# News product of the steady slots on VectorE instead of GpSimd: a recurrent network kernel

## Chip, cores and metric

The kernel runs on one core of a Trainium2 chip. The metric is the time of one execution in microseconds (us) on the device. Five engines work in order, each through its own list of instructions: TensorE (matmuls), VectorE and GpSimd (elementwise), ScalarE (activations) and SyncE (which only issues DMAs here). They meet at semaphores: an instruction behind `wait_ge(s, n)` starts once semaphore s has reached n, and `.then_inc(s, 1)` raises it when an instruction is complete. SBUF is the memory in which all engines but SyncE work on tiles of 128 partitions; PSUM, the tensor `ps` of eight banks, is where TensorE writes, and GpSimd does not use it.

## The reference

For 2048 rows with 50 time steps of 128 features, and one further vector `news` per row:

```
h_t  = GRU(x_t, h_{t-1})                      z, r = sigmoid(...), hc = tanh(xh + r*hh)
                                              h = z*h + (1-z)*hc
emb  = [h_t, news - h_t, news, h_t * news]
at   = sigmoid(relu(relu(emb W1 + b1) W2 + b2) W3 + b3)          attention score per step
g_t  = second GRU over h_t, its update gate multiplied by at:    u = sigmoid(...), r = sigmoid(...)
                                              c = tanh(xc + r*(g Uc)), g = (1 - at*u)*g + at*u*c
y    = sigmoid(dense(leaky(dense(leaky(batchnorm([g_T, news]) ...)))))
```

`h_t * news` is the product that the change is about.

## The kernel before

Features lie on the 128 partitions, and the 2048 rows are four chunks (NC) of 512 columns. An item is one chunk of one time step: 4 x 50 = 200 items, item i having chunk i % 4. Matmuls run in float16, each operand split into a high and a low part (`h_hi`, `h_lo`); a product of weights and data is three passes (high with high, high with low, low with high) over two halves of 64 output rows, six matmuls (`split_product`, L1149 and L1150 of `two_tiles`). ScalarE makes the high parts, GpSimd or VectorE the low ones by a subtraction.

The program is written as slots, by hand, for each engine. Slot `low` does the first GRU for item `low`, the first attention layer for item `low` - 2, and the second GRU for item `low` - 10 (LAG). Slots 4 to 13 are the function `early`; slots 14 (EARLY) to 199 are `slot`, the steady ones; after them ten slots of `late` finish the second GRU, and the dense layers end the kernel. In every fourth steady slot (17, 21, ... 197) TensorE also does the second attention layer (`attention_2`, L1232) and the scores (`scores`, L1223), and ScalarE and VectorE have work for these at the beginning of the slot behind (L575, L581, L856).

A steady slot, in order, on each engine, with the names by which the rows call the results:

- TensorE: attention layer 1 on h and on h*news (waits for `h_lo`, `hn_lo`), reset gate of item `low`, update gate of the second GRU (waits for the new h of item `low` - 1, which frees its bank), `xh`, second GRU's reset gate and its `ghh`, the update gate z, `gxh` (waits for the second state g), in every fourth slot the scores (`pe.wait_ge(gr_ready, late(LAG))`: their bank is the one that `gr` is read from) and the second attention layer, then `hh` of a later item.
- ScalarE: [relu and high part of the second attention layer], candidate of the second GRU L662, `h_hi` L502, `r` L647, `a_hi` L512, `hn_hi` L507, `gu` L676, `x_hi` L527, `hc` L686, `g_hi` L690, `gr` L693, z L696.
- VectorE: [`a_lo` L856], `ps` L861 (attention plus its share of the news), `ps` L879, [`a_lo` L856], `t` L988 (waits for r), `ps` L885 (waits for `gus`), `t` L998, `g` L890, `a_lo` L867, `gt` L1027 (waits for gr), `ps` L1033 (waits for `d` and z), `gt` L1038, `h` L1041, the new state of item `low`. Then the next slot's list begins.
- GpSimd: `g_lo` L409, `hn` L327 of item `low` - 1 (`state_news`, waits for h), `gus` L416 (update gate times score), `hn_lo` L333 (waits for ScalarE's `hn_hi`), `h_lo` L339, `d` L423 (waits for hc), `x_lo` L346.
- SyncE: the loads of x for the next step and the rows of scores, each behind its semaphore.

`hn` has two buffers, one for even and one for odd items. In `late(ITEMS)`, the first slot behind the steady ones, GpSimd makes `gus` and then the `hn` of the last item, item 199, before `h_lo` and `hn_lo` of it.

Of the kernel before, what the change touches and what calls it, by code (L numbers as in the profile page):

```python
# [24 lines left out]
ALU = mybir.AluOpType  # L25
# [8 lines left out]
NC = 4  # L34
# [43 lines left out]
def rec_kernel(nc, xs, pack_gru, pack_state, pack_att, pack_rest, out):  # L78
# [21 lines left out]
    def has(item):  # L100
        return 0 <= item < ITEMS
# [26 lines left out]
    with ExitStack() as ctx:  # L128
# [187 lines left out]
        def _(pool):  # L316
# [4 lines left out]
            def state_news(item, count):  # L321

                c, k = item % NC, item % 2
                if isinstance(item, int) and item < NC:
                    pool.wait_ge(news_landed[c], 16)
                pool.wait_ge(h_ready, count)
                g.tensor_tensor(hn[:, k, :], h32[:, c, :], news[:, c, :], ALU.mult).then_inc(hn_ready, 1)  # L327
# [69 lines left out]
            def slot(s0, off):  # L397
                low = off + (s0 if isinstance(s0, int) else LOOP_LO)

                def at(lag):  # L400
                    return s0 + (off - lag + 1)

                def landed(lag):
                    return 4 * (s0 + (off - lag - (low - lag) % NC)) + 16

                if has(low - LAG - 4) and has(low - LAG - 4 + NC):
                    c = (low - LAG - 4) % NC
                    pool.wait_ge(ghi_ready, at(LAG + 4))
                    g.tensor_tensor(g_lo[:, c, :], g32[:, c, :], g_hi[:, c, :], ALU.subtract).then_inc(glo_ready, 1)  # L409
                if has(low - 1):  # L410
                    state_news(low - 1, at(1))
                if has(low - LAG - 1):
                    c, k = (low - LAG - 1) % NC, (low - LAG - 1) % 2
                    pool.wait_ge(gu_ready, at(LAG + 1))
                    pool.wait_ge(score_landed, landed(LAG + 1))
                    g.tensor_tensor(gus[:, k, :], gu[:, k, :], score[:, c, :], ALU.mult).then_inc(gus_ready, 1)  # L416
                if has(low - 1):
                    state_news_low(low - 1, at(1))
                    state_low(low - 1, at(1))
                if has(low):  # L420
                    c, k = low % NC, low % 2
                    pool.wait_ge(hc_ready, at(0))
                    g.tensor_tensor(d[:, k, :], h32[:, c, :], hc[:, k, :], ALU.subtract).then_inc(d_ready, EARLY + 1 if low == EARLY else 1)  # L423
                if has(low + 1) and low > EARLY:
                    input_low(low + 1, at(-1))
# [13 lines left out]
            def late(low):  # L439
                item = low - LAG  # L440
                if low == ITEMS:
                    gated_low(item - 4)
                if item >= ITEMS - LAG + 2:
                    pool.wait_ge(ge_ready, item - 2 - NC)
                gated_share(item - 1, item, 16 * ((item - 1) // NC + 1), score if item <= ITEMS - 2 * NC else late_scores[(item - 1) // NC - T + 2])
                if low == ITEMS:
                    state_news(ITEMS - 1, ITEMS)
                if low == ITEMS:
                    state_low(ITEMS - 1, ITEMS)
                    state_news_low(ITEMS - 1, ITEMS)  # L450
                    gated_low(item - 3)
                elif low <= SHORT + 1:
                    gated_low(item - 3 if low <= SHORT else item - 2)
                if SHORT <= low < LAST - 1 and low != SHORT + 1:
                    gated_low(item - 2)
                if ITEMS + 3 <= low < ITEMS + 3 + NC:
                    c = low - ITEMS - 3
                    pool.wait_ge(newshi_ready, c + 1)
                    g.tensor_tensor(news_lo[:, c, :], news[:, c, :], news_hi[:, c, :], ALU.subtract).then_inc(newslo_ready, 1)
                if low == ITEMS + 2:  # L460
                    pool.wait_ge(d1_half, 1)
                    g.tensor_tensor(d1_lo, dw1, d1_hi, ALU.subtract).then_inc(d1_split, 1)
                    pool.wait_ge(d2_half, 1)
                    g.tensor_tensor(d2_lo, dw2, d2_hi, ALU.subtract).then_inc(d2_split, 1)
# [349 lines left out]
        def _(dve):  # L814
# [152 lines left out]
            def slot(s0, off):  # L967
                low = off + (s0 if isinstance(s0, int) else LOOP_LO)

                def at(lag):  # L970
                    return s0 + (off - lag + 1)

                def late(lag):
                    return s0 + (off - lag + 1 - NC)

                if pairs_of(low - 1):
                    low_2(0, paired(s0 + (off - 1)))
                if has(low - 2):
                    attention_1_news(low - 2, at(2))
                if low > EARLY and has(low - LAG - 1):  # L980
                    gated_difference(low - LAG - 1, at(LAG + 1))
                if low > EARLY and pairs_of(low - 1):
                    low_2(1, paired(s0 + (off - 1)))
                if has(low):
                    k = low % 2
                    dve.wait_ge(hh_pe, late(0))
                    dve.wait_ge(r_ready, at(0))
                    v.scalar_tensor_tensor(out=t[:, k, :], in0=ps[:, B_HH, :], scalar=b_hs,  # L988
                                           in1=r[:, k, :], op0=ALU.add, op1=ALU.mult).then_inc(t1_ready, 1)
                if low == EARLY:  # L990
                    gated_first(low - LAG - 1, at(LAG + 1))
                elif has(low - LAG - 1):
                    gated_step(low - LAG - 1, at(LAG + 1))
                if has(low):
                    k = low % 2
                    dve.wait_ge(t1_ready, at(0))
                    dve.wait_ge(xh_pe, at(0))
                    v.tensor_tensor(t[:, k, :], t[:, k, :], ps[:, B_XH, :], ALU.add).then_inc(t2_ready, 1)  # L998
                if low == EARLY:
                    low_2(1, paired(low - 1))  # L1000
                if low > EARLY and has(low - LAG - 1):
                    gated_state(low - LAG - 1, at(LAG + 1))
                if has(low - 2):
                    attention_1_low(low - 2, at(2))
                known = low if isinstance(s0, int) else None
                if known == BN_LO:
                    bn_eps()
                if known == BN_LO + 1:
                    bn_guess()
                for i in range(NEWTON):  # L1010
                    if known == BN_LO + 3 * i + 2:
                        bn_square(i)
                    if known == BN_LO + 3 * i + 3:
                        bn_error(i)
                    if known == BN_LO + 3 * i + 4:
                        bn_root(i)
                if known == BN_LO + 3 * NEWTON + 2:
                    bn_scale()
                if known == BN_LO + 3 * NEWTON + 3:
                    bn_mean()  # L1020
                if known == BN_LO + 3 * NEWTON + 4:
                    bn_shift()
                if has(low - LAG):
                    k = (low - LAG) % 2
                    dve.wait_ge(ghh_pe, late(LAG))
                    dve.wait_ge(gr_ready, late(LAG))
                    v.tensor_tensor(gt[:, k, :], gr[:, k, :], ps[:, B_GHH, :], ALU.mult).then_inc(gt1_ready, 1)  # L1027
                if known == BN_LO:
                    bn_shift_bits()
                if has(low):  # L1030
                    dve.wait_ge(d_ready, at(0))
                    dve.wait_ge(z_ready, at(0))
                    v.tensor_tensor(ps[:, B_Z, :], d[:, low % 2, :], ps[:, B_Z, :], ALU.mult).then_inc(e_ready, 1)  # L1033
                if has(low - LAG):
                    k = (low - LAG) % 2
                    dve.wait_ge(gxh_pe, at(LAG))
                    dve.wait_ge(gt1_ready, late(LAG))
                    v.tensor_tensor(gt[:, k, :], gt[:, k, :], ps[:, B_GXH, :], ALU.add).then_inc(gt2_ready, 1)  # L1038
                if has(low):
                    dve.wait_ge(e_ready, at(0))  # L1040
                    v.tensor_tensor(h32[:, low % NC, :], hc[:, low % 2, :], ps[:, B_Z, :], ALU.add).then_inc(h_ready, 1)  # L1041

            dve.wait_ge(gru_landed, 16)
            v.tensor_tensor(b_zr[:, :], gru_b[:, 0:2], gru_b[:, 3:5], ALU.add).then_inc(b_ready, 1)
# [543 lines left out]
```

## Time and profile before

| | |
|---|---|
| time, median of 3 runs | 1918.23 us (1917.87 to 1918.46) |
| the profiled execution: its own time | 1917.94 us |
| its span | 1916.1 us |
| granted TensorE clock | 1.0 of full |
| busy PE / DVE / ACT / POOL | 1908.0 / 1473.6 / 1471.6 / 1645.4 us |
| hn L327 on POOL | 200 times, mean 1275 ns |
| h L1041 on DVE | 186 times, mean 681 ns |

The profile calls the engines PE (TensorE), PEld (its weight loads), DVE (VectorE), ACT (ScalarE), POOL (GpSimd) and SP (SyncE). Busy time is time in which an instruction of the engine is being executed, as the record of start and end has it; a time in which the instruction waits within the engine for something that is no semaphore counts as busy. An engine at 77% with others at 100% says nothing by itself: what matters is whose wait ends last at the place in question.

### The profile page before, as it was taken

Reading aid. Unit: us, or ns where it says so; the run is one execution under the profiler, and the core shown is the slowest. Engines: PE = TensorE matmul, PEld = TensorE weight load, DVE = VectorE, ACT = ScalarE, POOL = GpSimd, SP = SyncE. Lnnn points to the kernel's source line nnn. Section 1 sums busy time; section 2 is a strip of 40 time slices with the busy share of each in tenths; the row PEclk is TensorE's granted clock in tenths of the full one; section 3 lists DMA queues with packets and bytes.
Section 4 is the critical chain, followed back from the end, with each engine's and each line's share of the span. In section 5 each row is a group of like instructions: output and inputs, shape, how many; then the busy total and the mean of one; then the engine's idle time right before and its main releaser. Section 6 shows DMA issues by size and latency. Waiting matters only on the chain.

```text
span 1916.1 us, 44510 instructions
## 1 busy us (share of the span) xinstructions
PE 1908.0 (100%) x17607; PEld 999.3 (52%) x17607; DVE 1473.6 (77%) x2324; ACT 1471.6 (77%) x2484; POOL 1645.4 (86%) x1409
## 2 busy tenths in 40 slices
PE   9999999999999999999999999999999999999999
PEld 4555555555555555555555555555555555555554
DVE  7777777777777777777777777777777777787777
ACT  7877777777777777777777777777777777777777
POOL 7888888888888888888888888888888888888886
PEclk9999999999999999999999999999999999999999
DMA  4211121112111211121121112111211121112110
GB/s 131 69 55 53 55 69 54 51 51 73 51 51 51 73 51 50 54 70 50 51 69 55 50 51 73 51 54 53 70 53 51 51 73 51 51 51 73 45 46 23
DMA packets 37911, 110.67 MB, mean 58 GB/s; under 512 B 4348, under 2 KB 4732, under 8 KB 31304
## 3 DMA queue, kind: packets, MB, share of 16 engines
q1 hardware_dynamic: 37560, 107.57, 17.4%
q8 instruction: 140, 2.29, 0.5%
q14 instruction: 67, 0.55, 0.1%
q10 hardware_dynamic: 144, 0.26, 0.1%
HBM read 107.40 MB, written 0.42 MB: 56 GB/s over the span
## 4 chain that ended last, share of the span: by engine, by line
PE 94%; ACT 2%; DVE 1%; POOL 1%; issue 1%; DMA 0%; SPq 0%; DVEq 0%; ACTq 0%; POOLq 0%
PE ps L1149 88%; PE ps L1232 3%; PE ps L1150 1%; PE ps L1223 1%; POOL hn_lo L333 0%; POOL h_lo L339 0%; DMA x<-in_xs 0%; DVE ps L885 0%; DVE ps L879 0%; ACT ps L752 0%; POOL hn L327 0%; ACT ps L575 0%; ACT g_hi L736 0%; ACT a_hi L512 0%; DVE g L890 0%
## 5 line engine op out<-in xcount | busy, mean ns | idle before, releaser
L1149 PE MATMUL ps<-h_hi,w_hi 128*64 128x512 f16 x1384 | 524.6, 379 | 1.9 <-POOL h_lo L339 1.4
L1150 PE MATMUL ps<-h_hi,w_hi 128*64 128x512 f16 x1384 | 524.7, 379 | 0.0
L1150 PE MATMUL ps<-h_lo,w_hi 128*64 128x512 f16 x1384 | 524.5, 379 | 0.0
L1150 PE MATMUL ps<-h_hi,w_lo 128*64 128x512 f16 x1384 | 524.5, 379 | 0.0
L1149 PE MATMUL ps<-h_hi,w_lo 128*64 128x512 f16 x1384 | 524.5, 379 | 0.0
L1149 PE MATMUL ps<-h_lo,w_hi 128*64 128x512 f16 x1384 | 524.5, 379 | 0.0
L333 POOL TENSOR_TENSOR hn_lo<-hn,hn_hi 128x512 f16<-128x512 f32 x200 | 232.4, 1162 | 162.2 <-ACT hn_hi L507 161.8
L327 POOL TENSOR_TENSOR hn<-h,news 128x512 f32<-128x512 f32 x200 | 255.0, 1275 | 74.3 <-DVE h L1041 74.3
L662 ACT ACTIVATE ps<-gt,p_rest 128x512 f32<-128x512 f32 x185 | 127.7, 690 | 199.4 <-DVE gt L1038 199.4
L346 POOL TENSOR_TENSOR x_lo<-x,x_hi 128x512 f16<-128x512 f32 x196 | 226.9, 1158 | 11.8 <-ACT x_hi L527 11.8
L416 POOL TENSOR_TENSOR gus<-gu,score 128x512 f32<-128x512 f32 x186 | 237.0, 1274 | 0.0
L423 POOL TENSOR_TENSOR d<-h,hc 128x512 f32<-128x512 f32 x186 | 236.8, 1273 | 0.0
L1027 DVE TENSOR_TENSOR gt<-gr,ps 128x512 f32<-128x512 f32 x186 | 128.0, 688 | 138.5 <-ACT gr L693 138.5
L339 POOL TENSOR_TENSOR h_lo<-h,h_hi 128x512 f16<-128x512 f32 x200 | 233.2, 1166 | 0.4 <-ACT h_hi L502 0.3
L1149 PE MATMUL ps<-x_hi,w_hi 128*64 128x512 f16 x605 | 229.3, 379 | 0.6 <-DVE a_lo L856 0.6
L1150 PE MATMUL ps<-x_hi,w_hi 128*64 128x512 f16 x605 | 229.3, 379 | 0.0
L1149 PE MATMUL ps<-x_lo,w_hi 128*64 128x512 f16 x605 | 229.3, 379 | 0.0
L1150 PE MATMUL ps<-x_lo,w_hi 128*64 128x512 f16 x605 | 229.3, 379 | 0.0
L1149 PE MATMUL ps<-x_hi,w_lo 128*64 128x512 f16 x605 | 229.3, 379 | 0.0
L1150 PE MATMUL ps<-x_hi,w_lo 128*64 128x512 f16 x605 | 229.3, 379 | 0.0
L1149 PEld LDWEIGHTS ps<-h_hi,w_hi 128*64 128x64 f16 x1384 | 152.2, 110 | 146.1 <-issue 3.0
L1149 PE MATMUL ps<-g_hi,w_hi 128*64 128x512 f16 x596 | 225.9, 379 | 1.1 <-DVE g_lo L1097 1.1
(191 smaller groups left out, 6756.4 us busy)
## 6 DMA issues: line engine op xcount, KB each, us to landing
x<-in_xs SPq DMA_DIRECT2D x199, 256.0 KB, 3.0
score<-score_rows SPq DMA_DIRECT2D x48, 1024.0 KB, 4.7
news<-in_xs SPq DMA_DIRECT2D x4, 256.0 KB, 5.3
x<-score_rows SPq DMA_DIRECT2D x1, 1024.0 KB, 4.6
h<-score_rows SPq DMA_DIRECT2D x1, 1024.0 KB, 5.1
score_rows<-s_rows SPq DMA_DIRECT2D x50, 8.0 KB
p_rest<-in_pack_rest SPq DMA_DIRECT2D x1, 776.0 KB, 7.0
p_att<-in_pack_att SPq DMA_DIRECT2D x1, 291.0 KB, 5.3
```

What stands on the lines that cost most here:

```text
L327: g.tensor_tensor(hn[:, k, :], h32[:, c, :], news[:, c, :], ALU.mult).then_inc(hn_ready, 1)
L333: g.tensor_tensor(hn_lo[:, item % NC, :], hn[:, k, :], hn_hi[:, item % NC, :], ALU.subtract).then_inc(hnlo_ready, 1)
L339: g.tensor_tensor(h_lo[:, item % HIST, :], h32[:, c, :], h_hi[:, item % HIST, :], ALU.subtract).then_inc(hlo_ready, 1)
L346: g.tensor_tensor(x_lo[:, c, :], x32[:, c, :], x_hi[:, c, :], ALU.subtract).then_inc(xlo_ready, 1)
L416: g.tensor_tensor(gus[:, k, :], gu[:, k, :], score[:, c, :], ALU.mult).then_inc(gus_ready, 1)
L423: g.tensor_tensor(d[:, k, :], h32[:, c, :], hc[:, k, :], ALU.subtract).then_inc(d_ready, EARLY + 1 if low == EARLY else 1)
L662: a.activation(ps[:, B_GXH, :], gt[:, (low - LAG - 1) % 2, :], ACT.Tanh, bias=b_gated[:, 2:3]).then_inc(gc_ready, 1)
L1027: v.tensor_tensor(gt[:, k, :], gr[:, k, :], ps[:, B_GHH, :], ALU.mult).then_inc(gt1_ready, 1)
L1149: m.matmul(ps[0:H, bank, :], weights[:, 0:H], moving, start=start, stop=stop)
L1150: return m.matmul(ps[H:P, bank, :], weights[:, H:P], moving, start=start, stop=stop)
L1223: done = m.matmul(ps[p * H:(p + 1) * H, bank, :], w3_pair[:, :], part[:, p, :], start=part is a2_hi, stop=part is a2_lo)
L1232: done = m.matmul(ps[k * H:(k + 1) * H, B_PAIR[p], :], w[:, A_2, 0:H], a1[:, 2 * p + k, :], start=w is w_hi and a1 is a1_hi, stop=a1 is a1_lo)
```

## The change

In the steady slots 14 to 199 VectorE multiplies the state with the news. The product stands directly behind the new state h of the same slot, so it is that of item `low` in slot `low`, where GpSimd made that of item `low` - 1. GpSimd keeps the products up to that of item 13, which it makes in slot 14; items 14 to 199, 186 of them, are VectorE's, item 199 in slot 199. VectorE waits for the low part of item `low` - 2 (it frees the buffer of hn), and for its own h.

```diff
@@ GpSimd, slot
-                if has(low - 1):
+                if low == EARLY:
                     state_news(low - 1, at(1))
@@ GpSimd, late
-                if low == ITEMS:
-                    state_news(ITEMS - 1, ITEMS)
                 if low == ITEMS:
                     state_low(ITEMS - 1, ITEMS)
                     state_news_low(ITEMS - 1, ITEMS)
@@ VectorE, slot
                 if has(low):
                     dve.wait_ge(e_ready, at(0))
                     v.tensor_tensor(h32[:, low % NC, :], hc[:, low % 2, :], ps[:, B_Z, :], ALU.add).then_inc(h_ready, 1)
+                    if low == EARLY:
+                        dve.wait_ge(hn_ready, low)
+                    dve.wait_ge(hnlo_ready, at(2))
+                    dve.wait_ge(h_ready, at(0))
+                    v.tensor_tensor(hn[:, low % 2, :], h32[:, low % NC, :], news[:, low % NC, :], ALU.mult).then_inc(hn_ready, 1)
```

## Rows read from the trace of the kernel before

**Rows 1.** The page, part 1: busy us (share of the span) xinstructions.

```profile
PE 1908.0 (100%) x17607; PEld 999.3 (52%) x17607; DVE 1473.6 (77%) x2324; ACT 1471.6 (77%) x2484; POOL 1645.4 (86%) x1409
```

**Rows 2.** Waits of TensorE, longest: waiter <- releaser: us in total, times, longest us.

```profile
PE ps L1149 <- POOL h_lo L339: 1.4, 1, 1.4
```

**Rows 3.** Chain that ended last: start us, us, what; first and last of 46 such pieces.

```profile
122.92 1.29 PE ps L1232 x12
...
1832.32 1.29 PE ps L1232 x12
```

**Rows 4.** Timeline of VectorE: start us, us, engine, line, operation, out<-in [idle before <-releaser].

```profile
1017.40 0.68 DVE L1041 TENSOR_TENSOR h<-hc,ps 128x512 f32<-128x512 f32 x1
1018.02 0.70 DVE L861 TENSOR_TENSOR ps<-c_news,ps 128x512 f32<-128x512 f32 x1
...
1020.12 0.75 DVE L988 SCALAR_TENSOR_TENSOR t<-ps,p_gru,r 128x512 f32<-128x512 f32 x1 [0.80 <-ACT r L647]
...
1021.38 0.68 DVE L998 TENSOR_TENSOR t<-t,ps 128x512 f32<-128x512 f32 x1
...
1024.01 0.69 DVE L1027 TENSOR_TENSOR gt<-gr,ps 128x512 f32<-128x512 f32 x1 [0.75 <-ACT gr L693]
...
1025.86 0.68 DVE L1038 TENSOR_TENSOR gt<-gt,ps 128x512 f32<-128x512 f32 x1
1026.46 0.68 DVE L1041 TENSOR_TENSOR h<-hc,ps 128x512 f32<-128x512 f32 x1
```

**Rows 5.** Timeline of GpSimd in the same slot.

```profile
1018.16 1.27 POOL L327 TENSOR_TENSOR hn<-h,news 128x512 f32<-128x512 f32 x1 [0.40 <-DVE h L1041]
1019.39 1.27 POOL L416 TENSOR_TENSOR gus<-gu,score 128x512 f32<-128x512 f32 x1
1021.08 1.16 POOL L333 TENSOR_TENSOR hn_lo<-hn,hn_hi 128x512 f16<-128x512 f32 x1 [0.42 <-ACT hn_hi L507]
1022.20 1.16 POOL L339 TENSOR_TENSOR h_lo<-h,h_hi 128x512 f16<-128x512 f32 x1
1023.32 1.27 POOL L423 TENSOR_TENSOR d<-h,hc 128x512 f32<-128x512 f32 x1
1024.55 1.15 POOL L346 TENSOR_TENSOR x_lo<-x,x_hi 128x512 f16<-128x512 f32 x1
1025.67 1.16 POOL L409 TENSOR_TENSOR g_lo<-g,g_hi 128x512 f16<-128x512 f32 x1
```

**Rows 6.** Timelines of head and tail: VectorE's two-tensor operations and GpSimd's beside them.

```profile
19.61 1.27 POOL L327 TENSOR_TENSOR hn<-h,news 128x512 f32<-128x512 f32 x1
...
20.05 1.38 DVE L1056 TENSOR_TENSOR x_lo<-x,x_hi 128x512 f16<-128x512 f32 x1 [1.42 <-ACT x_hi L527]
...
20.84 1.60 POOL L339 TENSOR_TENSOR h_lo<-h,h_hi 128x512 f16<-128x512 f32 x1
...
1900.52 0.61 POOL L468 CAST a_hi<-r 128x512 f16<-128x512 f32 x1
...
1900.53 1.14 DVE L1097 TENSOR_TENSOR g_lo<-g,g_hi 128x512 f16<-128x512 f32 x1 [0.19 <-ACT g L737]
```

**Rows 7.** Timeline of VectorE, two operations, the second waiting for the first.

```profile
79.33 0.69 DVE L955 TENSOR_TENSOR d<-d,ps 128x512 f32<-128x512 f32 x1
80.06 0.69 DVE L957 TENSOR_TENSOR h<-d,ps 128x512 f32<-128x512 f32 x1
```

**Rows 8.** Timeline of ScalarE in the slot of rows 4.

```profile
1019.90 0.59 ACT L512 ACTIVATE a_hi<-ps 128x512 f16<-128x512 f32 x1
1020.38 0.63 ACT L507 ACTIVATE hn_hi<-hn 128x512 f16<-128x512 f32 x1
...
1022.09 0.72 ACT L686 ACTIVATE hc<-t,p_gru 128x512 f32<-128x512 f32 x1
...
1023.24 0.67 ACT L693 ACTIVATE gr<-ps,p_rest 128x512 f32<-128x512 f32 x1
```

**Rows 9.** Timeline of TensorE: the first score matmuls of the slot behind.

```profile
1034.00 0.38 PE L1223 MATMUL ps<-a_hi,w_pair 128*64 128x512 f16 x2
```

## The prediction

> **What bounds the kernel now.** I read the busy table first: TensorE is busy for 1908.0 of 1916.1 us, so at most 8.1 us of the span are anything but matmuls [rows 1]. Next the waits: the longest that TensorE has is 1.4 us, once, for an h_lo [rows 2]; the slots of the loop appear in none of its rows. The chain repeats every four slots: the twelve score-layer matmuls stand in it from 122.92 to 1832.32 us, 46 times, which is 1709.40 / 45 = 37.99 us for four slots [rows 3]. A plain slot takes 9.06 us (the new h from 1017.40 to 1026.46) [rows 4]; the fourth, in which TensorE has the second attention layer and the scores besides, takes 37.99 - 3 x 9.06 = 10.8. I call it the score slot. The change can win something only in head or tail; in the loop it can lose, if a ring of waits over the other engines becomes longer than 37.99.
>
> **What is removed.** GpSimd loses 186 multiplications (items 14 to 199) of 1.27 us, and with each the wait for h: h ends at 1018.08, hn starts at 1018.16 [rows 4, 5]. That is 236 us of GpSimd time, none of it in the chain of the loop. The one that GpSimd makes in slot 14 stays. The last one, behind the steady slots, brought h_lo and hn_lo of one item up to 1.2 us later; TensorE did not wait there, so the gain lies between 0 and 1.4 us (its longest wait, rows 2). I take 0.
>
> **What is added.** VectorE gets one 128x512 multiplication per slot, of two SBUF operands. Its operations in the loop take 0.68 to 0.75 and start some 0.60 apart [rows 4]. Taken at 0.60 it would be hidden: t starts at 1020.12, set by the reset gate; from h at 1017.40 come h, ps, ps at 0.62, 0.60 and 0.60, so 0.9 us before t were free, of which 0.3 would be left. No DMA is added and none is moved.
>
> But no operation of VectorE in the loop reads two SBUF tensors, since one operand always lies in ps, and the few of head and tail that do are the slow ones [rows 6]. At 20.05 VectorE's x_lo begins while GpSimd's hn runs to 20.88; it ends at 21.43, so it takes 1.38, and ends 0.55 behind the end of GpSimd's operation. GpSimd's next, h_lo, begins in the record at 20.84, later than VectorE's, and takes 1.60 instead of 1.16: it stood behind VectorE. At 1900.53 VectorE asks 0.01 behind a cast of 0.61 that GpSimd began at 1900.52, and takes 1.14: it stood behind the cast. Who comes first goes first, and the other waits for the whole operation. The Trainium skill says it so too (SBUF — State Buffer, "SBUF: two separate sides": the port pair that the two share is an exclusive lock for the whole instruction, also against a VectorE operation with two SBUF inputs); the trace agrees, with 0.55 us behind the end. By another of its rules (GPSIMD Engine Reference, "Engine selection": elementwise work on a tile belongs on VectorE, GpSimd being about twice as slow) the result would be the hidden 0.60 and no change; its ratio fits 1.27 against 0.68 here, but the shared port is not in it.
>
> **Who comes first.** GpSimd has no late input between g_lo and gus, so gus starts 1.11 us behind g_lo (as g_lo behind x_lo, 1024.55 to 1025.67, rows 5). In an undisturbed slot g_lo starts 9.06 before 1025.67, at 1016.61, and gus at 1017.72. h starts at 1017.40, and an operation that waits for the one before it on VectorE starts 0.73 behind that one's start [rows 7]: hn comes at 1018.13. gus is first by 0.4 us and runs to 1018.99. hn ends 0.55 later, at 1019.54, and the operation behind it may start 0.08 before that, 0.47 behind the end of gus (0.60 behind the start of a 0.68 operation is the same 0.08).
>
> From a start of gus, G, two chains run to the next slot's race.
> To the next gus: gus 1.27, 0.47, ps 0.70, handoff 0.03, a_hi to hn_hi 0.48, hn_hi 0.63, handoff 0.07, then on GpSimd without a gap hn_lo, h_lo, d, x_lo, g_lo: 1.12 + 1.12 + 1.23 + 1.12 + 1.11 [rows 4, 5, 8]. Sum 9.35.
> To the next hn: 1.27 + 0.47, two ps of 0.60, t to the second t 1.26, that t 0.68, handoff 0.03, hc to gr 1.15, gr 0.67, handoff 0.10, three starts of 0.60 up to h, 0.73 [rows 4, 7, 8]. Sum 9.36.
> Both are 0.3 longer than the slot, and they end within some 0.02 us of each other. This is where the prediction is decided. Where gus leads again, the next slot begins 0.3 later still. Where hn leads, it waits only for the rest of g_lo, about 0.5 us are spent instead of 1.7, and the delay is gone.
>
> In the first slot gus leads by 0.4; in the second by 0.1 (there h is still held by the update gate of TensorE's time); from the third on by 0.02 or so. I let gus win: nothing that it waits for is late, while hn passes three semaphores, and 0.73 is the shortest that rows 7 allow for one.
>
> **The sum.** In the slot behind a score slot TensorE's extra 1.7 us let the ring catch up, and there its longest way is through hc: 1.27 + 0.47, four starts (a_lo, ps, ps, a_lo) at 0.60, t to second t 1.26, 0.68, 0.03, hc 0.72, handoff 0.08, d, x_lo, g_lo 1.23 + 1.12 + 1.11, sum 10.37 [rows 4, 5, 8]. The ring of four slots is 3 x 9.35 + 10.37 = 38.42, against TensorE's 37.99: 0.43 us each, wherever TensorE is caught by it. It is caught first by the scores at 1034.00 [rows 9], which need gr: gr ended 9.06 behind 1023.24 + 0.67, at 1032.97. After the change G of the score slot is 1017.72 + 9.06 + 0.6 = 1027.38, and gr ends 1.27 + 0.47 + 1.20 + 1.26 + 0.68 + 0.03 + 1.15 + 0.67 = 6.73 later, at 1034.11, past its deadline. The ring then closes, and TensorE stands still for just as much as it is too long. The rounding of ten handoffs puts 0.43 between 0.4 and 0.5; I take 0.45. 46 x 0.45 = 20.7 us. The profiled execution took 1917.94 us for its span of 1916.1, and stands 0.29 under the median of 1918.23; 1917.94 + 20.7 = 1938.6, on the median's scale 1938.9. I forecast 1939.
>
> **Bounds.** A ring has some ten handoffs, each read to 0.02, and the blocked operation's 0.55 rests on two cases: 0.45 may be 0.15 or 0.8, so 7 to 37 us, 1925 to 1955 for this case.
>
> **Rivals.**
> *hn wins the late races, no change.* A lead of 0.02 us can fall the other way. For it: the two sums are equal within their reading. Against it: the semaphores. If hn leads in the score slot or in the one before, the delay never passes 0.3 there, TensorE's slack of 1.0 us at the scores (1034.00 less 1032.97) holds, and the time is 1918 to 1920. It decides from 0.03 us. A block shorter than rows 6 show, or none at all (0.30 for the race, 0.05 for this), would end in the same time, as the 0.60 is then hidden in the 0.9 ahead of t. Together 0.35.
> *A longer ring, much slower.* If each own semaphore adds 0.05 and a blocked operation 0.1, a plain slot of the ring takes 9.5: 3 x 9.5 + 10.55 = 39.05, 1.06 x 46 = 49 us, 1967. For it: GpSimd's five operations and the chain of VectorE leave no gap to hide such additions in. Against it: rows 6 fit 0.55 to the hundredth. 0.07.
> *Faster.* GpSimd's freed time ends a wait of TensorE in the tail: 1.4 us at most, 1916.8, and that is within the 0.2% (3.8 us) under which a measurement of this kernel can't be told from no change. For more, over half of the 8.1 us that are not matmuls would have to go, and most lie ahead of slot 14: 0.02.
>
> The forecast has 0.56. Slower by over 0.2% is 0.56 + 0.07, less 0.02 for a ring that is too long by under 0.08 us: 0.61. Within 0.2%: 0.37. Faster: 0.02. The range goes from the rival without change to the upper part of my case, 1917.5 to 1950.
>
> **What would show it.** VectorE's new multiplication has a mean of 1.4 us or so, not 0.69; gus starts 1.11 behind g_lo, and hn's record ends 0.55 behind that of gus. TensorE waits some 46 times, 0.3 to 0.6 us, for gr of ScalarE ahead of the scores, and the score-layer matmuls stand 38.4 us apart. I am wrong if they stay 37.99 apart; then in one slot of four hn stands ahead of gus and takes under 1.2 us. If hn takes 0.69 throughout, the port is not shared as rows 6 have it.

## The result, and the profile after

The changed kernel takes 1940.64 us (median of 4 runs, 1939.61 to 1942.03), the kernel before 1918.05 beside it: ratio 1.0116, 95% interval 1.0104 to 1.0128. The forecast was 1939. The profiled execution took 1942.03 us, span 1940.2. One execution of the version with an operand in PSUM, further down, took 2511.11 us at a granted clock of 0.753 and is left out of the ratio there. So the change makes the kernel slower, by 22.6 us, and this is how its profile answers the rows of before.

Part 1 of the page, to be read against [rows 1]:

```profile
PE 1918.9 (99%) x17607; PEld 996.9 (51%) x17607; DVE 1749.1 (90%) x2510; ACT 1468.3 (76%) x2484; POOL 1411.5 (73%) x1223
```

VectorE has 186 operations more, but its busy time grew by 275.5 us, 1.48 for each. GpSimd lost 234. The waits of the whole kernel (waiter, releaser: us in total, times, longest) show where TensorE is caught; [rows 2] had nothing of the steady slots:

```profile
POOL hn_lo L333 <- ACT hn_hi L505: 481.2, 194, 3.1
ACT ps L660 <- DVE gt L1036: 207.3, 139, 2.3
DVE gt L1025 <- ACT gr L691: 130.1, 172, 0.9
ACT a_hi L510 <- DVE ps L859: 114.9, 149, 1.6
...
PEld ps L1226 <- ACT gr L691: 35.0, 46, 0.9
PE ps L1226 <- ACT gr L691: 12.9, 45, 0.4
```

The scores' weight loads wait 46 times for gr of ScalarE. Neither figure is the loss: PEld's counts a stretch in which the array still works on earlier matmuls, PE's only the gap behind their modelled ends. The loss is read from the distance of the same instruction, the first weight load of the scores: 122.11 to 1831.50 us before, 125.10 to 1855.80 after, 45 cycles each, so 37.99 and 38.46 us. That is 21.3 us.

Before:

```profile
122.11 0.11 PEld L1223 LDWEIGHTS ps<-a_hi,w_pair 128*64 128x64 f16 x2
...
1831.50 0.11 PEld L1223 LDWEIGHTS ps<-a_hi,w_pair 128*64 128x64 f16 x2
```

After (the figure in brackets is idle time ahead, and what ended it):

```profile
125.10 0.11 PEld L1226 LDWEIGHTS ps<-a_hi,w_pair 128*64 128x64 f16 x2 [0.88 <-ACT gr L691]
...
1855.80 0.11 PEld L1226 LDWEIGHTS ps<-a_hi,w_pair 128*64 128x64 f16 x2 [0.76 <-ACT gr L691]
```

Timelines of VectorE and GpSimd in a score slot, the one behind it, and two plain ones (start us, us, engine, line, operation):

```profile
1002.15 0.68 DVE L1039 TENSOR_TENSOR h<-hc,ps 128x512 f32<-128x512 f32 x1
1002.93 1.77 DVE L1044 TENSOR_TENSOR hn<-h,news 128x512 f32<-128x512 f32 x1
1004.63 0.68 DVE L859 TENSOR_TENSOR ps<-c_news,ps 128x512 f32<-128x512 f32 x1
1005.22 0.69 DVE L877 TENSOR_TENSOR ps<-ps,g 128x512 f32<-128x512 f32 x1
1005.82 0.74 DVE L986 SCALAR_TENSOR_TENSOR t<-ps,p_gru,r 128x512 f32<-128x512 f32 x1
...
1012.29 1.79 DVE L1044 TENSOR_TENSOR hn<-h,news 128x512 f32<-128x512 f32 x1
...
1022.87 1.58 DVE L1044 TENSOR_TENSOR hn<-h,news 128x512 f32<-128x512 f32 x1
...
1032.04 1.77 DVE L1044 TENSOR_TENSOR hn<-h,news 128x512 f32<-128x512 f32 x1
```

```profile
1001.75 1.17 POOL L409 TENSOR_TENSOR g_lo<-g,g_hi 128x512 f16<-128x512 f32 x1
1002.87 1.28 POOL L416 TENSOR_TENSOR gus<-gu,score 128x512 f32<-128x512 f32 x1
1006.53 1.17 POOL L333 TENSOR_TENSOR hn_lo<-hn,hn_hi 128x512 f16<-128x512 f32 x1 [2.38 <-ACT hn_hi L505]
...
1012.25 1.29 POOL L416 TENSOR_TENSOR gus<-gu,score 128x512 f32<-128x512 f32 x1
...
1019.16 1.28 POOL L423 TENSOR_TENSOR d<-h,hc 128x512 f32<-128x512 f32 x1 [0.26 <-ACT hc L684]
...
1022.63 1.27 POOL L416 TENSOR_TENSOR gus<-gu,score 128x512 f32<-128x512 f32 x1
...
1031.99 1.27 POOL L416 TENSOR_TENSOR gus<-gu,score 128x512 f32<-128x512 f32 x1
```

ScalarE between the two, in the first of these slots:

```profile
1005.34 0.60 ACT L510 ACTIVATE a_hi<-ps 128x512 f16<-128x512 f32 x1 [1.05 <-DVE ps L859]
1005.84 0.62 ACT L505 ACTIVATE hn_hi<-hn 128x512 f16<-128x512 f32 x1
```

gus begins 0.06, 0.04, 0.24 and 0.05 us ahead of hn. hn's record then ends 0.55 behind that of gus (1004.70 against 1004.15), as the blocked operations of [rows 6], and the next operation starts 0.48 behind it. There is no idle time between hn and t; the 0.80 that [rows 4] had ahead of t is gone. GpSimd, relieved of a seventh of its work (234 of 1645 us), spends it waiting 2.4 us for hn_hi. This is a ring: gus holds hn, hn holds ps and with it ScalarE's a_hi and hn_hi, hn_hi holds hn_lo and GpSimd's list, and at its end stands the next gus. In the slot behind the score slot its longest way is through hc, for which d waits (0.26). From one gus to the next it takes 9.38, 10.38, 9.36 and (1041.36 - 1031.99) 9.37 us.

TensorE at the place where the ring catches it, in the same slot (the scores' first matmuls; the number before the arrow is idle time ahead):

```profile
1009.66 0.41 PE L1226 MATMUL ps<-a_hi,w_pair 128*64 128x512 f16 x2 [0.27 <-ACT gr L691]
```

```profile
1009.65 0.11 PEld L1226 LDWEIGHTS ps<-a_hi,w_pair 128*64 128x64 f16 x2 [0.75 <-ACT gr L691]
```

Outside the loop little is left: behind the last score load of the loop come 84.6 us before and 84.4 after. Ahead of the first one the profiled run after is 3.0 us later. Of this, 2.1 stands already at 10.29 us against 8.16 (the first weight load of x_hi), in code that both kernels share and far ahead of the first changed slot, so it isn't the change; 2.2 stands at 101.60 against 99.44, and the other 0.8 comes in before the first scores, where the ring closes. That run is also 1.4 above its median. The medians are 22.6 apart, 21.3 of them the loop.

### The profile page after: what moved, and what is told of

The parts are those of the page before. It is cut to its first block and busy times, and to the rows that moved or that the text cites. A ratio compares the mean times of both kernels' runs of the same rounds, so it can differ in the third digit from the quotient of the medians.

```text
span 1940.2 us, 44696 instructions
## 1 busy us (share of the span) xinstructions
PE 1918.9 (99%) x17607; PEld 996.9 (51%) x17607; DVE 1749.1 (90%) x2510; ACT 1468.3 (76%) x2484; POOL 1411.5 (73%) x1223
## 5 line engine op out<-in xcount | busy, mean ns | idle before, releaser
L1044 DVE TENSOR_TENSOR hn<-h,news 128x512 f32<-128x512 f32 x186 | 315.5, 1696 | 19.4
```

The costliest lines, as they stand in the source:

```text
L1044: v.tensor_tensor(hn[:, low % 2, :], h32[:, low % NC, :], news[:, low % NC, :], ALU.mult).then_inc(hn_ready, 1)
```

## The experiments

The theory to be tested has three parts: VectorE's product meets gus at a shared port and waits for all of it; which of the two comes first decides; TensorE loses just what the ring is longer than 37.99 us. The rivals are that VectorE simply has too much to do, and that the late gr ahead of the scores is the cause by itself. All times are medians, each beside runs of the kernel before on the same chip (1918.0 to 1918.3).

**gus behind hn.** One wait added on GpSimd:

```diff
                     pool.wait_ge(score_landed, landed(LAG + 1))
+                    if has(low - 1):
+                        pool.wait_ge(hn_ready, at(1))
                     g.tensor_tensor(gus[:, k, :], ...)
```

(Dots within a line of a diff stand for arguments that are not shown.)

> GpSimd waits for hn of VectorE before it begins gus; nothing else differs from the changed kernel. Port order theory (a gus that begins just ahead of hn holds VectorE back for 1.27 us): hn then never meets gus, takes 0.69 instead of a mean 1.70, gus still ends before hn_hi is there, the four-slot ring falls back under TensorE's 37.99, time 1918 (1917 to 1920). Rival, load on VectorE (one more operation per slot is too much for an engine in line with the others): nothing changes for VectorE's count of operations, 1938 to 1942.

Measured 1918.41, ratio 1.0003 (0.9994 to 1.0012). The whole loss is gone with a wait more and not one operation less. VectorE's and GpSimd's timelines:

```profile
562.60 0.69 DVE L1046 TENSOR_TENSOR hn<-h,news 128x512 f32<-128x512 f32 x1
```

```profile
563.46 1.27 POOL L418 TENSOR_TENSOR gus<-gu,score 128x512 f32<-128x512 f32 x1 [1.28 <-DVE hn L1046]
```

hn takes 0.69, gus begins 1.28 us later than it could, and nobody waits for it. VectorE is at 83%, with the same 2510 operations as the changed kernel. Load on VectorE is refuted, and the order is shown to decide.

**One operand in PSUM.** The diff shows VectorE; TensorE's two waits for h become waits for hn, as said below it:

```diff
-                    v.tensor_tensor(hn[:, low % 2, :], h32[:, low % NC, :], news[:, low % NC, :], ALU.mult).then_inc(hn_ready, 1)
+                    v.tensor_tensor(hn[:, low % 2, :], h32[:, low % NC, :], ps[:, B_Z, :], ALU.mult).then_inc(hn_ready, 1)
```

> hn is h times the PSUM bank of z instead of h times news (the product with news is left out), so VectorE reads only one SBUF tensor; TensorE waits for hn instead of h before it reuses that bank. Port theory: no meeting with GpSimd at all though gus still begins first, hn 0.69, 1918 to 1920. Rival, load or order of VectorE's list: same operation count and size, 1938 to 1942.

Measured 1919.52, ratio 1.0009 (0.9999 to 1.0019). Here gus begins first and runs right through hn:

```profile
572.85 0.69 DVE L1044 TENSOR_TENSOR hn<-h,ps 128x512 f32<-128x512 f32 x1
```

```profile
572.39 1.27 POOL L416 TENSOR_TENSOR gus<-gu,score 128x512 f32<-128x512 f32 x1
```

Same place in the list, same size, and gus runs through the whole of hn (it leads by 0.46, where it led by 0.05 in the changed kernel); the second SBUF operand is gone, and with it the block, which was about 1.1 us in the changed kernel. So what is shared is the way to SBUF of a second operand. The Trainium skill gives this cause (SBUF — State Buffer, "Who interferes with whom": an instruction of VectorE with at most one SBUF input, outside the 2-port perf modes, doesn't contend with GpSimd, one with two contends with a GpSimd operation that reads); the two traces agree, 0.69 against 1.77 us.

**More work on GpSimd.** (The line that declares `idle` is not shown.)

```diff
+                    g.memset(idle[:, :], 0.0)
                     g.tensor_tensor(gus[:, k, :], ...)
```

> A fill of 128x128 (0.20 us in the trace) is added on GpSimd ahead of gus in each steady slot: GpSimd does more work. Port order theory: gus led hn by only 0.04 to 0.06 us in three of four slots, now it comes 0.1 or more behind it, hn waits only for the rest of g_lo or nothing, 1918 to 1921, faster than the changed kernel. Rival, a ring whose length is what counts whoever comes first: 4 x 0.17 longer per four slots, 1940.6 + 46 x 0.68 = 1972.

Measured 1921.43, ratio 1.0018 (1.0009 to 1.0028): 0.4 above the range that I gave, but 19 us faster than the changed kernel though GpSimd does more. The timelines show both outcomes of the race in turn:

```profile
562.53 0.69 DVE L1046 TENSOR_TENSOR hn<-h,news 128x512 f32<-128x512 f32 x1
571.56 1.51 DVE L1046 TENSOR_TENSOR hn<-h,news 128x512 f32<-128x512 f32 x1
580.66 0.69 DVE L1046 TENSOR_TENSOR hn<-h,news 128x512 f32<-128x512 f32 x1
```

```profile
562.64 1.72 POOL L418 TENSOR_TENSOR gus<-gu,score 128x512 f32<-128x512 f32 x1
...
571.25 1.26 POOL L418 TENSOR_TENSOR gus<-gu,score 128x512 f32<-128x512 f32 x1
...
580.75 1.73 POOL L418 TENSOR_TENSOR gus<-gu,score 128x512 f32<-128x512 f32 x1
```

In one slot hn leads by 0.11 and gus is the one that takes 1.72; in the next gus leads by 0.31 and hn takes 1.51. A slot in which hn leads gives the delay back, and as long as the two outcomes alternate, up to slot 183, four slots take 37.97 to 38.01 us (the first four 37.77), from the new h to the new h. The remaining 3 us (its loop is 1712.26 us for 45 cycles against 1709.39) stand at the end. From slot 184 to slot 197 VectorE has one more small operation in each slot, `bn_t` for the batchnorm, between a_lo and gt (in slot 184 two):

```profile
1789.05 1.64 DVE L1046 TENSOR_TENSOR hn<-h,news 128x512 f32<-128x512 f32 x1
...
1824.37 1.19 DVE L925 SCALAR_TENSOR_TENSOR bn_t<-bn_t,p_rest 128x2 f32<-128x2 f32 x1
1825.48 0.68 DVE L1027 TENSOR_TENSOR gt<-gr,ps 128x512 f32<-128x512 f32 x1
...
1828.05 1.65 DVE L1046 TENSOR_TENSOR hn<-h,news 128x512 f32<-128x512 f32 x1
```

```profile
1827.87 1.29 POOL L418 TENSOR_TENSOR gus<-gu,score 128x512 f32<-128x512 f32 x1
```

With it gt starts 1.71 behind a_lo (1823.77) instead of 1.44, so hn comes 0.27 later, and gus leads in every slot from 184 on, here by 0.18. Four slots then take 39.00 us (1789.05 to 1828.05). So the filler helps only while it turns the race; where gus wins all the same, it lengthens the ring, near the 38.46 + 0.68 = 39.14 of the rival.

**hn later in VectorE's list**, behind L877 of the next slot (that of the last item in the first slot of `late`), with no wait beyond its own:

> VectorE makes hn of item low - 1 in slot low behind ps L877, ahead of t, instead of directly behind h; no wait added. In the kernel before, the place ahead of t had 0.8 us idle and gus would be over by then. Port order theory: hn 0.69 and hidden in three of four slots, delays t by at most 0.3 in the slot behind a score slot, where TensorE gives 1.7 back; 1918 to 1920. Rival, load on VectorE: same load, 1938 to 1942.

Measured 1919.31, ratio 1.0006 (0.9996 to 1.0015). Its hn takes 0.68 from 565.36 on, gus having run from 563.86 to 565.13. The same operation on the same engine costs nothing in a place where GpSimd reads nothing.

**A semaphore in place of the port.** VectorE waits for gus:

```diff
+                    if low > EARLY:
+                        dve.wait_ge(gus_ready, at(LAG))
                     dve.wait_ge(hnlo_ready, at(2))
```

> VectorE waits by a semaphore until gus is complete before it begins hn; port order is then fixed, the meeting is gone and only the ring is left, with a handoff of 0.08 and a full start of 0.60 in place of the 0.47 behind gus: 0.21 longer per slot, 0.84 per four slots. Ring theory: TensorE stands for the ring's excess of 0.48 + 0.84 us, 46 x 1.32 = 61, so 1979 (1968 to 1985). Rival, the blocked port itself costs more than standing behind gus would: faster than 1940.

Measured 1973.96, ratio 1.0290 (1.0273 to 1.0307). The same order, made explicit, costs 33 us more than the port does:

```profile
570.17 0.69 DVE L1046 TENSOR_TENSOR hn<-h,news 128x512 f32<-128x512 f32 x1 [1.18 <-POOL gus L416]
570.78 0.69 DVE L859 TENSOR_TENSOR ps<-c_news,ps 128x512 f32<-128x512 f32 x1
```

```profile
568.86 1.27 POOL L416 TENSOR_TENSOR gus<-gu,score 128x512 f32<-128x512 f32 x1
```

L859 starts 0.65 behind the end of gus (570.78 less 570.13) where it started 0.48 behind it in the changed kernel: 0.17 a slot, not the 0.21 that I had put. Four times 0.17 is 0.68, on the excess of 0.47 makes 1.15; hn to hn over four slots is 598.78 - 559.62 = 39.16, an excess of 1.17, and 46 x 1.17 = 54 us are close to the 56 measured. The ring's length is what TensorE pays.

**A shorter hn.**

```diff
-                    v.tensor_tensor(hn[:, low % 2, :], h32[:, low % NC, :], news[:, low % NC, :], ALU.mult)...
+                    v.tensor_tensor(hn[:, low % 2, 0:448], h32[:, low % NC, 0:448], news[:, low % NC, 0:448], ALU.mult)...
```

> hn is made for 448 of its 512 columns (the last 64 are left out), everything else as in the changed kernel. Both chains of the race get shorter by 0.067 us, so gus still leads; the ring of four slots is shorter by 0.27 and its excess over TensorE's 37.99 falls from 0.48 to 0.21: 1918.2 + 46 x 0.21 = 1928 (1925 to 1931).

Measured 1928.9, ratio 1.0056 (1.0041 to 1.0071). The race is as before (gus at 574.94, hn at 574.99, 1.71 us), the loop is (1841.74 - 123.41) / 45 = 38.19 us by the scores' weight loads, where 38.46 - 0.27 = 38.19 was expected.

> hn for 256 of 512 columns (half is left out): the ring of four slots is shorter by 1.07, so below 37.99, though gus still holds hn back in most slots. Ring theory: a floor at the time of the kernel before, 1918 (1917 to 1919), with hn still blocked where gus leads. Rival, each microsecond of the block costs: half of the 22 us, 1929 or more.

Measured 1919.46, ratio 1.0006 (0.9997 to 1.0015). hn still stands behind gus:

```profile
571.94 1.19 DVE L1044 TENSOR_TENSOR hn<-h,news 128x256 f32<-128x256 f32 x1
```

Where nothing holds it, this form takes 0.42, so it ends 0.7 to 0.8 us late in the slots of the loop, and TensorE loses nothing: its loop is 1709.38 us. A block is free as long as the ring stays under TensorE's cycle. Cost by block alone is refuted.

**The scores later.** TensorE's six matmuls of `candidate_state` ahead of the scores instead of behind the second attention layer:

```diff
+                if has(low + 1):
+                    pe.wait_ge(t1_ready, at(0))
+                    candidate_state(low - NC + 1, at(NC - 1))
                 if score_of(low):
...
-                if has(low + 1):
-                    pe.wait_ge(t1_ready, at(0))
-                    candidate_state(low - NC + 1, at(NC - 1))
```

> The changed kernel, with TensorE's six matmuls for hh of a later item put ahead of the scores in every fourth slot, so that the scores begin 0.65 us later and their wait for gr has 0.65 more room. Ring theory: the wait for the scores only shows the ring's excess; with it relieved, TensorE is caught by the next wait (g or gu of the second GRU, or gr with the delay grown by 0.65) and the time stays at 1938 to 1944. Rival, the late gr ahead of the scores is the cause: its lateness of 0.45 us fits into 0.65, so 1918 to 1922.

> The same order of TensorE in the kernel before, to see what the order alone does: both theories 1917 to 1920, since no wait of TensorE had under 1 us of room there.

Measured 1942.66 (ratio 1.0125, 1.0110 to 1.0140) on the changed kernel and 1918.3 (1.0000, 0.9990 to 1.0009) on the one before. The waits of the weight loads, changed kernel with the new order:

```profile
PEld ps L1152 <- DVE g L888: 30.1, 125, 0.3
PEld ps L1152 <- ACT gu L674: 24.5, 102, 0.3
PEld ps L1226 <- ACT gr L691: 10.4, 45, 0.2
```

The wait at which TensorE was caught fell from 35.0 to 10.4 us, two others took its place, and the time did not fall (it is 2 us above that of the changed kernel, within the expected range). The late gr is a symptom.

## Why the prediction was right

- *What bounds it, and that nothing can be won in the loop*: right. Every version whose ring is short enough ends at 1918 to 1920, none below.
- *hn is blocked by gus, 0.55 behind its end*: right, 0.55 in the changed kernel. That the second SBUF operand does it was argued from rows of head and tail; the run with an operand in ps shows it.
- *Who comes first*: the outcome was right, and it was given only 0.56. The two chains were put at 9.35 and 9.36, equal within their reading, so that it came out this way is in part luck: the range, 1917.5 to 1950, took in the other outcome too. gus led by 0.04 to 0.06 in the late races, not 0.02. The term that was short is VectorE's wait for its own h: hn starts 0.78 behind h's start (1002.15 to 1002.93), where [rows 7] gave 0.73. That makes the second chain 9.41. The way in was forecast as leads of 0.4, 0.1 and 0.02; the first four races of the run have 0.98, 0.04, 0.05 and 0.03. The filler, which moves gus by 0.16 us, turns the race in every second slot up to slot 183.
- *The sum*: a ring of 38.42 was forecast, taken as 0.45 over TensorE's 37.99; measured 38.46, so 0.47. Its parts, gus to gus, were 9.35 and 10.37, measured 9.36 to 9.38 and 10.38. The 46 x 0.45 = 20.7 became 21.3 over 45 cycles and, in the profiled run, 0.8 us in the slots ahead of the first score; the remaining 0.5 of the 22.6 is not placed.
- *Where TensorE is caught*: right, 46 times at the scores, for gr. The text said that the place does not matter to the sum; the moved scores show that.
- *What it would look like*: hn's mean was forecast at 1.4 us and is 1.70. In the forecast's own terms a race lost by 0.02 makes hn wait for nearly all of gus, 1.25 + 0.55 = 1.80, and only one slot in four has the longer lead; I had averaged over the undisturbed slot's 0.4 instead. The time does not hang on it, since it is counted from gus. TensorE's wait was forecast at 0.3 to 0.6 us; the matmuls wait 0.29 on average (12.9 / 45), their weight loads 0.76 (35.0 / 46), and the loss per cycle, 0.47, lies between.
- *Faster, from the freed GpSimd*: right that there is nothing; the tail is 84.4 us against 84.6, and the version with gus behind hn, which frees GpSimd just as much, ends at 1918.41.
- *The rival without change* was a real alternative: it lay 0.04 to 0.06 us of order away, and one wait on GpSimd makes it true.

## What to carry to other kernels

Before an elementwise operation moves from GpSimd to VectorE, look at where its operands lie: with two in SBUF it waited here for the whole of a GpSimd operation that reads and had begun first, and the record shows that as busy time, not as a wait. Then close the ring, from the operation back to itself over all engines and over as many slots as the pattern repeats, and compare it with the cycle of the engine that bounds the kernel: under it a block is free, above it every hundredth is paid. If two engines meet within hundredths of a microsecond, fix the order by a semaphore on the side that has room; here that wait cost nothing, and the opposite one 56 us over the kernel before. A filler that only shifts the timing is no such fix: it held for most of the loop and failed in the last 16 slots, when VectorE's list had grown by a small operation.

## What the runs showed of the hardware

- Order at the port follows the start of the records: gus was ahead in every race of the changed kernel, by 0.03 us at the least (hn then took 1.78), and with the filler hn was ahead in 85 races, by 0.08 to 0.11, and gus took 1.71 to 1.74.
- A fill on GpSimd (562.48 to 562.68) did not hold back hn, which began at 562.53 and took 0.69, as in the 84 other slots in which hn began during the fill; it reads nothing.
- Standing behind the port is 0.17 us cheaper than waiting for the same operation by a semaphore, since the next operation of VectorE starts 0.48 behind the end of gus in place of 0.65.
- A VectorE operation that waits for the one ahead of it started 0.78 behind that one's start here, against 0.60 without the wait.
